# Perceiver layer on one core: group sums on ScalarE, context loads in pairs, a fifth-slot load in order of use, and the last two k-tiles by batch

## The chip, the cores and the metric

One Trainium2 chip, one core. The metric is device time of the whole program in microseconds, the median of several runs. The kernel is written out by hand: every engine has its own list of instructions, and semaphores tie the lists together.

## The reference, cut to what matters

Two batches of 128 rows with 2048 features go through three residual steps: a quantised product with a context, multi-query attention with 32 heads, and a linear layer with 4-bit weights in groups of 128 inputs.

```python
def _L0_xattn_ref(x1, x2, x1_scale, x1_zp, x2_scale, x2_zp):
    q1 = fake_quant(x1, x1_scale, x1_zp)
    q2 = fake_quant(x2, x2_scale, x2_zp)
    return jnp.matmul(q1, q2)

def _L0_attn_ref(hidden_states, Wq, Wkv, Wo):
    q = (hidden_states @ Wq).reshape(b, s, NUM_HEADS, HEAD_DIM)
    kv = hidden_states @ Wkv
    ...
    attn = jax.nn.softmax(scores, axis=-1)
    out = jnp.einsum('bhqk,bkd->bqhd', attn, v).reshape(b, s, h)
    return out @ Wo

def _L0_ffn_ref(x, qweight, qzeros, scales, bias):
    wq = qweight[:, None, :] >> shifts[None, :, None] & MASK
    wq = wq.reshape(IN_FEATURES, OUT_FEATURES)
    zq = _unpack4(qzeros, OUT_FEATURES) + 1
    W = scales[g_idx] * (wq - zq[g_idx]).astype(scales.dtype)
    return jnp.einsum('bsi,io->bso', x, W) + bias

x = x + _L0_xattn_ref(_layernorm(x), ctx_4096, ...)     # ctx_4096 is (2, 2048, 2048) f32
x = x + _L0_attn_ref(_layernorm(x), Wq, Wkv, Wo)
x = x + _L0_ffn_ref(_layernorm(x), qweight, qzeros, scales, bias)
```

## The kernel before, in words

The program has four stages, one after the other on TensorE.

**Context stage.** The context is 32 k-tiles of 128 rows by 2048 columns, 1 MiB each, 16 for each batch. SyncE loads them into a ring of eight slots (`ctx_slots`: four in `raw`, four in `ctx_more`; line 299), each as soon as ScalarE has rounded the tile that lay there (`ctx_q`). ScalarE rounds a tile to uint8 in `round_ctx` (L434), VectorE turns it into bf16 in `convert_ctx` (L699, two buffers `q16`), TensorE multiplies it in `ctx_tile` (L978, four products of 512 columns, and L985, four column sums). Between these ScalarE also quantises the rows of x (`quantise_rows`), and for batch 0, while batch 1 still streams, takes the square root for the second norm (`sqrt_of(2)`) and copies four transposed blocks out of PSUM (`upper(0, g)`, L447). After the last tile come the zero-point product, the residual, the norm and the transposes of batch 1 (`transposes(1)`, L1010).

**Query stage.** The products that want full f32 accuracy are made of three: each operand is split into an upper part (ScalarE, rounded to fp32r: `upper`, `upper_w`) and a remainder (VectorE: `remainder`, `remainder_w`), and TensorE computes upper x upper, upper x lower, lower x upper. The weights come in granules of 1 MiB (four k-tiles by 512 columns; `load_granule`), numbered `w`: 0 to 15 are Wq, 16 to 31 are Wo, 32 to 47 are the k-tiles of the linear layer. Attention for the eight (head group, batch) units runs between the granules of Wq (scores L1104, transposed probabilities L1116, values L1128, `heads_hi` L498 and `heads_lo` L830).

**Output stage.** Sixteen granules of Wo, `o_granule(i, b)` (L1017, L1018, L1019). Raw, upper and lower parts have five slots here; the fifth is `raw_fifth` with room in `xt`. The list `USED` has the granules in the order in which TensorE finishes them: 16, 17, 18, 20, 19, 21, ... TensorE runs `o_granule(4, 0)` (w = 20, fifth slot) before `o_granule(3, 0)` (w = 19), but the loads, ScalarE's upper parts and VectorE's remainders go 19, 20.

**Linear layer.** The weight is never built as a whole: VectorE unpacks two nibbles at a time (`nibbles(m)`, L878), ScalarE subtracts eight (`less_eight(m)`, L574), VectorE multiplies by the upper and the lower part of the scales (`ffn_upper(j)` L885, `ffn_lower(j)` L890), and TensorE runs `f_granule(j, b)`: for each k-tile j and batch b eight products by the upper part (`f_by_upper`) and four by the lower (`f_by_lower`), all in L1166. What the zero points and the bias add is one more product of eight (`correction`, L1199) of `corr_r` with `rsum`, the sums of the normed rows over each group of 128 inputs. Before, those sums come from TensorE: `row_sums` (L1160) multiplies the 16 transposed k-tiles of both parts with a 0/1 mask `group_of`, and VectorE and ScalarE combine and split the result (L945, L946, L594, L948). The normed rows lie in `work`, which is also where `nibbles(1)` and `nibbles(2)` write once the transposes have read it. `corr_split` is signalled when `corr_r` is made (L920).

The last lines of TensorE's list run k-tiles 12 to 15 for batch 0 and then for batch 1, the last of each with one bank after the other finished, so that VectorE can add (L959) and SyncE can store (L345).

## Time and profile before

| | before |
|---|---|
| median of 3 runs | 416.29 us (416.13 to 417.54) |
| the profiled execution | 416.08 us |
| its span in the profile | 414.3 us |
| mean granted TensorE clock | 0.984 of full |
| TensorE busy | 369.8 us (89%) |
| VectorE busy | 315.9 us (76%) |
| ScalarE busy | 222.6 us (54%) |
| GpSimd busy | 18.9 us (5%) |
| HBM read | 74.91 MB |

The profile is of one execution. Busy time of matmuls is modelled and overlaps by up to 0.17 us from one to the next, so the distance between two starts is the better price. The shares of busy time are means over stages that have different limits; the rows further down are taken stage by stage.

### The profile page before, as it was taken

Reading aid. Unit: us, or ns where it says so; the run is one execution under the profiler, and the core shown is the slowest. Engines: PE = TensorE matmul, PEld = TensorE weight load, DVE = VectorE, ACT = ScalarE, POOL = GpSimd, SP = SyncE. Lnnn points to the kernel's source line nnn. Section 1 sums busy time; section 2 is a strip of 40 time slices with the busy share of each in tenths; the row PEclk is TensorE's granted clock in tenths of the full one; section 3 lists DMA queues with packets and bytes.
Section 4 is the critical chain, followed back from the end, with each engine's and each line's share of the span. In section 5 each row is a group of like instructions: output and inputs, shape, how many; then the busy total and the mean of one; then the engine's idle time right before and its main releaser. Section 6 shows DMA issues by size and latency. Waiting matters only on the chain.

```text
span 414.3 us, 4696 instructions
## 1 busy us (share of the span) xinstructions
PE 369.8 (89%) x1828; PEld 269.2 (65%) x1828; DVE 315.9 (76%) x359; ACT 222.6 (54%) x266; POOL 18.9 (5%) x51
## 2 busy tenths in 40 slices
PE   0167768779899999999999999999999999999996
PEld 0112223227687777777877777888888788888884
DVE  2598989858853693783984977995999899999922
ACT  1898988986344576576675735544524433333000
POOL 6000000008000000000020000000000000000000
PEclk9998986999999999999999999999999999999999
DMA  8999999997173594685349421967200000000033
GB/s 324 422 424 422 415 425 422 416 400 283 27 277 115 184 223 122 209 180 173 130 142 277 139 95 53 356 224 277 111 0 0 2 0 0 2 0 2 0 101 101
DMA packets 24274, 77.44 MB, mean 187 GB/s; under 512 B 1626, under 2 KB 1802, under 8 KB 19210
## 3 DMA queue, kind: packets, MB, share of 16 engines
q1 hardware_dynamic: 24084, 77.01, 51.4%
q8 instruction: 14, 0.23, 0.3%
q10 hardware_dynamic: 168, 0.13, 0.1%
q14 instruction: 8, 0.07, 0.1%
HBM read 74.91 MB, written 2.10 MB: 186 GB/s over the span
## 4 chain that ended last, share of the span: by engine, by line
PE 71%; DVE 12%; DMA 10%; ACT 3%; issue 2%; ACTq 0%; DVEq 0%
PE bank L1166 20%; PE bank L1017 12%; PE bank L1019 12%; PE bank L1018 12%; DMA ctx_more<-in_ctx 9%; DVE q L699 3%; ACT q L434 2%; PE bank L1030 2%; PE bank L1128 2%; PE bank L1104 2%; DVE stats L613 2%; PE bank L1116 1%; PE bank L1040 1%; DMA prm_row<-in_L_xattn_x_zp 1%; PE bank L1010 1%
## 5 line engine op out<-in xcount | busy, mean ns | idle before, releaser
L456 ACT ACTIVATE w_hi<-raw 128x2048 fp32r<-128x2048 f32 x29 | 55.4, 1914 | 35.9 <-DMA raw<-in_L_attn_Wo 15.7
L643 DVE TENSOR_TENSOR w_lo<-raw,w_hi 128x2048 fp32r<-128x2048 f32 x27 | 61.6, 2286 | 11.2 <-ACT w_hi L456 11.2
L978 PE MATMUL bank<-q,at 128*128 128x512 bf16 x128 | 39.4, 438 | 15.0 <-DVE q L699 14.5
L1166 PE MATMUL bank<-w_hi,hd 128*128 128x512 f32 x208 | 52.6, 390 | 0.0
L1166 PEld LDWEIGHTS bank<-w_hi,hd 128*128 128x128 f32 x208 | 39.0, 188 | 8.0
L699 DVE TENSOR_SCALAR q<-q 128x2048 bf16<-128x2048 uint8 x32 | 38.4, 1217 | 5.4 <-ACT q L434 2.8
L1017 PE MATMUL bank<-w_hi,hd 128*128 128x512 f32 x104 | 41.2, 396 | 0.0
L1019 PE MATMUL bank<-w_hi,hd 128*128 128x512 f32 x104 | 40.5, 390 | 0.0
L1018 PE MATMUL bank<-w_lo,hd 128*128 128x512 f32 x104 | 40.5, 389 | 0.0
L1017 PE MATMUL bank<-w_hi,xt 128*128 128x512 f32 x96 | 39.6, 412 | 0.0
L1019 PE MATMUL bank<-w_hi,xt 128*128 128x512 f32 x96 | 37.6, 392 | 0.0
L1018 PE MATMUL bank<-w_lo,xt 128*128 128x512 f32 x96 | 37.5, 390 | 0.0
L485 ACT ACTIVATE work<-work,neg_mx 128x128 f32<-128x128 f32 x64 | 24.8, 389 | 23.4 <-DVE neg_mx L811 23.3
L434 ACT ACTIVATE q<-raw,prm,inv 128x2048 uint8<-128x2048 f32 x16 | 33.1, 2091 | 3.3 <-DMA raw<-in_ctx 3.3
L434 ACT ACTIVATE q<-ctx_more,prm,inv 128x2048 uint8<-128x2048 f32 x16 | 33.0, 2089 | 3.0 <-DMA ctx_more<-in_ctx 3.0
L978 PEld LDWEIGHTS bank<-q,at 128*128 128x128 bf16 x128 | 11.1, 106 | 34.8 <-DVE q L699 18.3
L574 ACT ACTIVATE work<-work 128x4096 bf16<-128x4096 uint16 x5 | 18.1, 3617 | 21.2 <-DVE work L878 21.2
L1166 PE MATMUL bank<-w_lo,hd 128*128 128x512 f32 x104 | 28.8, 389 | 0.0
L803 DVE SCALAR_TENSOR_TENSOR work<-kq,bank 128x128 f32<-128x128 f32 x64 | 13.3, 280 | 17.6 <-PE bank L1104 17.6
L1017 PEld LDWEIGHTS bank<-w_hi,hd 128*128 128x128 f32 x104 | 19.5, 188 | 4.9 <-issue 0.8
L1017 PEld LDWEIGHTS bank<-w_hi,xt 128*128 128x128 f32 x96 | 18.0, 188 | 6.5 <-issue 2.6
L1019 PEld LDWEIGHTS bank<-w_hi,hd 128*128 128x128 f32 x104 | 19.5, 188 | 4.2
(157 smaller groups left out, 618.8 us busy)
## 6 DMA issues: line engine op xcount, KB each, us to landing
raw<-in_ctx SPq DMA_DIRECT2D x16, 1024.0 KB, 17.1
ctx_more<-in_ctx SPq DMA_DIRECT2D x16, 1024.0 KB, 17.7
raw<-in_L_attn_Wq SPq DMA_DIRECT2D x16, 1024.0 KB, 5.7
raw<-in_L_attn_Wo SPq DMA_DIRECT2D x13, 1024.0 KB, 5.1
raw_fifth<-in_L_attn_Wo SPq DMA_DIRECT2D x3, 1024.0 KB, 7.2
resid<-in_x SPq DMA_DIRECT2D x2, 1024.0 KB, 11.7
scale<-in_L_ffn_scales SPq DMA_DIRECT2D x16, 128.0 KB, 6.1
packed<-in_L_ffn_qweight SPq DMA_DIRECT2D x2, 1024.0 KB, 7.1
```

The costliest lines, as they stand in the source:

```text
L434: nc.scalar.activation(q8[:, i % Q8], ctx_slots[i % CTX_RING], ACT.Identity, bias=prm[:, 3:4], scale=inv[:, 2:3]).then_inc(ctx_q, 1)
L456: nc.scalar.activation(hi_slots[s], raw_slots[s], ACT.Copy).then_inc(w_hi_set, 1)
L485: ins = nc.scalar.activation(prob[:, c], prob[:, c], ACT.Exp, scale=-1.0, bias=neg_mx[:, u % 2, h:h + 1], accum_out=den[:, u % 2, h:h + 1])
L574: nc.scalar.activation(values.bitcast(BF16), values.bitcast(U16), ACT.Copy, bias=-8.0).then_inc(d8_set, 1)
L643: nc.vector.tensor_tensor(lo_slots[s], raw_slots[s], hi_slots[s].bitcast(F32), ALU.subtract).then_inc(w_lo_set, 1)
L699: nc.vector.tensor_scalar(q16[:, i % 2], q8[:, i % Q8], -QSHIFT, None, ALU.add).then_inc(ctx_c, 1)
L803: ins = nc.vector.scalar_tensor_tensor(out=prob[:, c], in0=kq[:], scalar=-sl[2 * PAIRS * g + r], in1=bank[:, SCORE_BANK + r % 2, r // 2 * ...
L978: mm(bank[:, 4 * b + n, :], at[:, k, b * P:(b + 1) * P], q16[:, i % 2, n * CH:(n + 1) * CH], start=start, stop=False)
L1017: mm(bank[:, out_bank, :], x_hi, hi[:, c], start=first, stop=False)
L1018: mm(bank[:, out_bank, :], x_hi, lo[:, c], start=False, stop=False)
L1019: return mm(bank[:, out_bank, :], x_lo, hi[:, c], start=False, stop=last)
L1166: return mm(bank[:, 4 * b + n, :], left[:, j, b * P:(b + 1) * P], right[slot_of(W_F + j)][:, n * CH:(n + 1) * CH], start=part == 0 and j = ...
```

## The change

It has five parts.

1. **Group sums.** `row_sums` with its mask goes. ScalarE now copies each group of 128 columns of the normed rows onto itself with a running sum (`group_sums`), 16 instructions for each batch, then writes that batch's 16 sums twice more into the columns of the second and third block. TensorE transposes the two 128x128 arrays (`sums_transposed`), VectorE splits the result. GpSimd makes two columns of ones in place of the mask.
2. **Order at the start of the linear layer.** Batch 1 of k-tiles 0 to 2 is done for three of the four banks first, since bank 7 receives the sums; the fourth chunk follows when the sums have been read. `nibbles(1)` moves ahead into `packed[:, 1]`, whose own load therefore waits for k-tile 3's lower part; `corr_r` is made earlier.
3. **Context in pairs.** Two k-tiles a transfer, 2 MiB: partition p of pair t takes rows 2p and 2p+1, so each partition's piece is 16 KiB in one run in place of 8 KiB. The transposes of `a16` take every second column to match. The last pair goes as two single transfers.
4. **Fifth slot.** The loads, the upper parts and the remainders of Wo follow `USED`: w = 20 before w = 19.
5. **Last k-tiles.** Only k-tiles 14 and 15 run batch by batch at the end.

```diff
+        group_sum = sb("group_sum", [P, B, P], F32)
-        nib_slots = [nib_a[:], work[:, 0], work[:, 1]]
+        nib_slots = [nib_a[:], packed[:, 1], work[:, 0]] + [(nib_a[:], work[:, 1], work[:, 0])[m % 3]
+                                                           for m in range(3, NPAIR)]
+        ctx_pair_slots = [t[:, s:s + 2] for t in (raw, ctx_more) for s in (0, 2)]
...
+        def sum_copies(b):
+            return group_sum[:, b, CBLK:3 * CBLK].rearrange("p (k c) -> p k c", k=2)[:, :, 0:GROUPS]
+        def sums_twice(b):
+            return group_sum[:, b, 0:GROUPS].unsqueeze(1).to_broadcast([P, 2, GROUPS])
...
-            for i in range(CTX_TILES):
-                if i == 6:
+            for i in range(CTX_TILES // 2 - 1):
+                s = i % len(ctx_pair_slots)
+                if i == 3:
                     sp.dma_start(resid[:, 1, :], x[1]).then_inc(x_loaded[1], 16)
-                if i >= CTX_RING:
-                    sp.wait_ge(ctx_q, i - CTX_RING + 1)
-                sp.dma_start(ctx_slots[i % CTX_RING], ctx_tiles[i]).then_inc(ctx_loaded[i % CTX_RING], 16)
+                if 2 * i >= CTX_RING:
+                    sp.wait_ge(ctx_q, 2 * i - CTX_RING + 2)
+                sp.dma_start(ctx_pair_slots[s], ctx_pairs[i]).then_inc(ctx_loaded[s], 16)
+            for e in range(2):
+                i = CTX_TILES - 2 + e
+                sp.wait_ge(ctx_q, i - CTX_RING + 1)
+                sp.dma_start(ctx_slots[i % CTX_RING], ctx_pairs[i // 2, :, e]).then_inc(ctx_last[e], 16)
...
-                load_granule(wo_rows, W_O, w)
+                load_granule(wo_rows, W_O, USED[w])
...
+            sp.wait_ge(f_lo_set, 4)
             sp.dma_start(packed[:, 1, :], qweight[P:2 * P, :]).then_inc(packed_loaded[1], 16)
...
+            def group_sums(b, groups):
+                for g in groups:
+                    rows = work[:, b, g * GROUPSIZE:(g + 1) * GROUPSIZE]
+                    ins = nc.scalar.activation(rows, rows, ACT.Copy, accum_out=group_sum[:, b, g:g + 1])
+                if g == GROUPS - 1:
+                    ins.then_inc(rs_sum, 1)
+                    act.wait_ge(rs_sum, b + 1)
+                    nc.scalar.activation(sum_copies(b), sums_twice(b), ACT.Copy).then_inc(rs_rows, 1)
+
             less_eight(0)
+            less_eight(1)
             sqrt_of(4)
             for g in range(4):
                 upper(2, g)
-            less_eight(1)
+            act.wait_ge(masks_set, 1)
+            group_sums(0, range(12))
             sqrt_of(5)
+            group_sums(0, range(12, GROUPS))
             for g in range(4):
                 upper(3, g)
-            act.wait_ge(rs_sum, 1)
-            nc.scalar.activation(rsum_t.bitcast(F32R), rtmp, ACT.Copy).then_inc(rs_set, 1)
-            for m in range(2, NPAIR):
+            group_sums(1, range(GROUPS))
+            less_eight(2)
+            for m in range(3, NPAIR):
                 less_eight(m)
...
-            dve.wait_ge(rs_done, 1)
-            link(nc.vector.tensor_scalar(rtmp, bank[:, 7, 0:B * P], one_row[:], None, ALU.add))
-            nc.vector.tensor_tensor(rtmp, bank[:, 7, B * P:2 * B * P], rtmp, ALU.add).then_inc(rs_sum, 1)
-            dve.wait_ge(rs_set, 1)
-            nc.vector.scalar_tensor_tensor(out=rsum[:], in0=rsum_t, scalar=part_lo[:, 1:2], in1=rtmp,
-                                           op0=ALU.mult, op1=ALU.add).then_inc(rs_out, 1)
             for j in range(3, KT):
                 ffn_upper(j)
+                if j == 3:
+                    dve.wait_ge(rs_done, 1)
+                    nc.vector.tensor_copy(rsum_t.bitcast(F32R), bank[:, 7, 0:B * P]).then_inc(rs_set, 1)
+                    dve.wait_ge(rs_set, 1)
+                    nc.vector.scalar_tensor_tensor(out=rsum[:], in0=rsum_t, scalar=part_lo[:, 1:2],
+                                                   in1=bank[:, 7, 0:B * P], op0=ALU.mult,
+                                                   op1=ALU.add).then_inc(rs_out, 1)
                 ffn_lower(j)
...
-            def row_sums():
-                pe.wait_ge(masks_set, 3)
+            def sums_transposed():
+                pe.wait_ge(rs_rows, B)
                 pe.wait_ge(lo_out, 4 * B + UNITS + 8)
-                for k in range(KT):
-                    ins = mm(bank[:, 7, :], group_of[:, k // PACK, :], hd[:, :, k, :], start=k == 0, stop=k == KT - 1)
+                for b in range(B):
+                    ins = nc.tensor.transpose(bank[:, 7, b * P:(b + 1) * P], group_sum[:, b, :], ident[:])
                 ins.then_inc(rs_done, 1)
...
-            f_by_upper(2, 0, (0,))
-            row_sums()
-            f_by_upper(2, 0, (1,))
+            f_by_upper(2, 0)
+            f_granule(0, 1, range(NCH - 1))
             f_by_lower(2, 0)
-            pe.wait_ge(rs_sum, 1)
-            f_granule(0, 1)
+            f_granule(1, 1, range(NCH - 1))
+            sums_transposed()
+            f_granule(2, 1, range(NCH - 1))
             pe.wait_ge(rs_out, 1)
+            for j in range(3):
+                f_granule(j, 1, range(NCH - 1, NCH))
             pe.wait_ge(corr_split, 1)
             correction()
-            f_granule(1, 1)
-            f_granule(2, 1)
-            for j in range(3, KT - 4):
+            for j in range(3, KT - 2):
                 f_granule(j, 0)
                 f_granule(j, 1)
             for b in range(B):
-                for j in range(KT - 4, KT - 1):
-                    f_granule(j, b)
+                f_granule(KT - 2, b)
                 f_last_granule(b)
```

How the lists change at three places. First TensorE, behind the transposes of batch 1's normed rows (`transposes(3)`), from the second of k-tile 2's products for batch 0 on. L1166 and L1190 are the linear layer's products, L1160 the group sums by product, L1184 the transposes of the sums, L1199 and L1223 the correction. Before:

```order
L1166 MATMUL bank<-w_hi,hd 128x512 x3
L1160 MATMUL bank<-hd,group_of 128x512 [waits lo_out,masks_set]
L1160 MATMUL bank<-hd,group_of 128x512 x15
L1166 MATMUL bank<-w_hi,hd 128x512 [waits lo_out,f_hi_set]
L1166 MATMUL bank<-w_hi,hd 128x512 x3
L1166 MATMUL bank<-w_lo,hd 128x512 [waits f_lo_set]
L1166 MATMUL bank<-w_lo,hd 128x512 x3
L1166 MATMUL bank<-w_hi,hd 128x512 [waits lo_out,f_hi_set,rs_sum]
```

After:

```order
L1190 MATMUL bank<-w_hi,hd 128x512 x7
L1190 MATMUL bank<-w_hi,hd 128x512 [waits lo_out,f_hi_set]
L1190 MATMUL bank<-w_hi,hd 128x512 x5
L1190 MATMUL bank<-w_lo,hd 128x512 [waits f_lo_set]
L1190 MATMUL bank<-w_lo,hd 128x512 x2
L1190 MATMUL bank<-w_lo,hd 128x512 [waits f_lo_set]
L1190 MATMUL bank<-w_lo,hd 128x512 x3
L1190 MATMUL bank<-w_hi,hd 128x512 [waits lo_out,f_hi_set]
L1190 MATMUL bank<-w_hi,hd 128x512 x5
L1190 MATMUL bank<-w_lo,hd 128x512 [waits f_lo_set]
L1190 MATMUL bank<-w_lo,hd 128x512 x2
L1184 MATMUL bank<-ident,group_sum 128x128 [waits lo_out,rs_rows]
```

Sixteen products of 512 columns, which stood behind four products of k-tile 2, are gone; two transposes stand behind thirty products.

Second, ScalarE from the first `less_eight` on (L574 and L583; L447 and L454 copy transposed blocks, L427 and L431 take the square root, L597 sums a group, L601 writes the copies). Before:

```order
L574 ACTIVATE nib_a<-nib_a 128x4096 [waits nib_set]
L427 ACTIVATE sd<-mv,eps_col 128x1 [waits var_set]
L447 ACTIVATE hd<-bank 128x4x128 [waits tr_done] x4
L574 ACTIVATE work<-work 128x4096 [waits nib_set]
L427 ACTIVATE sd<-mv,eps_col 128x1 [waits var_set]
L447 ACTIVATE hd<-bank 128x4x128 [waits tr_done] x4
L594 ACTIVATE k_t<-kv_t 128x256 [waits rs_sum]
L574 ACTIVATE work<-work 128x4096 [waits nib_set]
```

After:

```order
L583 ACTIVATE nib_a<-nib_a 128x4096 [waits nib_set]
L583 ACTIVATE packed<-packed 128x4096 [waits nib_set]
L431 ACTIVATE sd<-mv,eps_col 128x1 [waits var_set]
L454 ACTIVATE hd<-bank 128x4x128 [waits tr_done] x4
L597 ACTIVATE work,group_sum<-work 128x128 [waits masks_set]
L597 ACTIVATE work,group_sum<-work 128x128 x11
L431 ACTIVATE sd<-mv,eps_col 128x1 [waits var_set]
L597 ACTIVATE work,group_sum<-work 128x128 x4
L601 ACTIVATE group_sum<-group_sum 128x2x16 [waits rs_sum]
L454 ACTIVATE hd<-bank 128x4x128 [waits tr_done] x4
L597 ACTIVATE work,group_sum<-work 128x128 x16
L601 ACTIVATE group_sum<-group_sum 128x2x16 [waits rs_sum]
```

The second `less_eight` has moved ahead of the transposes; 32 sums and two copies stand behind them.

Third, VectorE between the last four attention units (L803 and L824 add the position bias, L811 and L832 find the maxima, L643 and L664 are remainders of weights). Before:

```order
L811 TENSOR_REDUCE neg_mx<-work 128x8 [waits score_out]
L643 TENSOR_TENSOR w_lo<-raw,w_hi 128x2048 [waits w_hi_set]
L803 SCALAR_TENSOR_TENSOR work<-kq,bank 128x128 [waits pt_done,score_done]
L803 SCALAR_TENSOR_TENSOR work<-kq,bank 128x128 x7
L811 TENSOR_REDUCE neg_mx<-work 128x8 [waits score_out]
L816 RECIPROCAL rden<-den 128x8 [waits exp_done]
L818 TENSOR_TENSOR work<-work,rden 128x1024 [waits dve_step]
L643 TENSOR_TENSOR xt<-raw_fifth,xt 128x2048 [waits w_hi_set]
```

After:

```order
L832 TENSOR_REDUCE neg_mx<-work 128x8 [waits score_out]
L664 TENSOR_TENSOR xt<-raw_fifth,xt 128x2048 [waits w_hi_set]
L824 SCALAR_TENSOR_TENSOR work<-kq,bank 128x128 [waits pt_done,score_done]
L824 SCALAR_TENSOR_TENSOR work<-kq,bank 128x128 x7
L832 TENSOR_REDUCE neg_mx<-work 128x8 [waits score_out]
L837 RECIPROCAL rden<-den 128x8 [waits exp_done]
L839 TENSOR_TENSOR work<-work,rden 128x1024 [waits dve_step]
L664 TENSOR_TENSOR w_lo<-raw,w_hi 128x2048 [waits w_hi_set]
```

The remainder of the fifth-slot granule and that of granule 19 have changed places.

## Rows read from the trace of the kernel before

**Rows 1.** Busy time by stretch: us, each engine's busy (count), granted clock, DMA, GB/s

```profile
44.00:93.40 49.40, 37.22 (x212) 13.05 (x212) 41.48 (x49) 44.26 (x26) 0.00 (x0) 0.90 1.02 416
127.00:250.00 123.00, 121.88 (x655) 92.38 (x654) 83.69 (x123) 76.04 (x177) 2.13 (x2) 1.00 0.57 168
```

**Rows 2.** The chain of waits in order of time: start, us, what

```profile
51.34 17.74 DMA ctx_more<-in_ctx
...
88.98 2.10 ACT q L434
...
334.25 74.13 PE bank L1166 x327
```

**Rows 3.** ScalarE's timeline, context stage: start, us, line, operation, idle before and releaser

```profile
45.17 6.14 ACT L434 ACTIVATE q<-ctx_more,prm,inv 128x2048 uint8<-128x2048 f32 x3
51.70 2.09 ACT L434 ACTIVATE q<-raw,prm,inv 128x2048 uint8<-128x2048 f32 x1 [0.39 <-DMA raw<-in_ctx]
...
71.59 2.10 ACT L434 ACTIVATE q<-raw,prm,inv 128x2048 uint8<-128x2048 f32 x1 [0.40 <-DMA raw<-in_ctx]
73.60 1.06 ACT L447 ACTIVATE xt<-bank 128x512 fp32r<-128x512 f32 x2
74.55 2.09 ACT L434 ACTIVATE q<-raw,prm,inv 128x2048 uint8<-128x2048 f32 x1
...
97.13 1.92 ACT L456 ACTIVATE w_hi<-raw 128x2048 fp32r<-128x2048 f32 x1 [0.80 <-DMA raw<-in_L_attn_Wq]
99.83 1.92 ACT L456 ACTIVATE w_hi<-raw 128x2048 fp32r<-128x2048 f32 x1 [0.77 <-DMA raw<-in_L_attn_Wq]
```

**Rows 4.** TensorE's timeline in the output stage, at the first fifth-slot granule

```profile
238.58 0.50 PE L1017 MATMUL bank<-xt,hd 128*128 128x512 f32 x1 [1.04 <-DVE xt L643]
```

**Rows 5.** VectorE's timeline, the remainders of granules 19 and 20

```profile
229.84 2.28 DVE L643 TENSOR_TENSOR w_lo<-raw,w_hi 128x2048 fp32r<-128x2048 f32 x1
236.24 2.28 DVE L643 TENSOR_TENSOR xt<-raw_fifth,xt 128x2048 fp32r<-128x2048 f32 x1
```

**Rows 6.** TensorE's timeline, start of the linear layer

```profile
320.13 1.95 PE L1010 MATMUL bank<-ident,work 128*128 128x128 f32 x16
321.84 1.17 PE L1166 MATMUL bank<-w_hi,hd 128*128 128x512 f32 x4
324.03 3.87 PE L1160 MATMUL bank<-hd,group_of 128*128 128x512 f32 x16 [1.02 <-DVE hd L634]
327.74 1.07 PE L1166 MATMUL bank<-w_hi,hd 128*128 128x512 f32 x4
```

**Rows 7.** VectorE's timeline, same place, and one `nibbles` further on

```profile
321.40 2.48 DVE L634 TENSOR_TENSOR hd<-bank,hd 128x512 fp32r<-128x512 f32 x4 [0.25 <-ACT hd L447]
323.80 2.28 DVE L890 TENSOR_TENSOR w_lo<-work,scale 128x2048 fp32r<-128x2048 bf16 x1
...
338.58 1.22 DVE L878 TENSOR_SCALAR nib_a<-packed 128x2048 int32<-128x2048 int32 x1
```

**Rows 8.** ScalarE's timeline: two of the exponentials with a sum, and batch 1's upper parts

```profile
200.39 0.40 ACT L485 ACTIVATE work<-work,neg_mx 128x128 f32<-128x128 f32 x1 [6.23 <-DVE neg_mx L811]
200.70 0.19 ACT L485 ACTIVATION_READ_ACCUMULATOR work<-work,neg_mx 128x1 f32 x1
200.79 0.39 ACT L485 ACTIVATE work<-work,neg_mx 128x128 f32<-128x128 f32 x1
...
320.77 2.07 ACT L447 ACTIVATE hd<-bank 128x512 fp32r<-128x512 f32 x4 [3.85 <-PE bank L1010]
```

**Rows 9.** TensorE by stretch: us, busy (count), granted clock, DMA, GB/s

```profile
39.20:42.40 3.20, 3.20 (x14) 0.50 1.02 425
...
60.00:70.00 10.00, 8.52 (x28) 0.51 1.01 421
```

**Rows 10.** TensorE's timeline around these stretches, and at `transposes(1)`

```profile
60.46 1.86 PE L978 MATMUL bank<-q,at 128*128 128x512 bf16 x4 [1.37 <-DVE q L699]
...
104.56 2.07 PE L1010 MATMUL bank<-ident,work 128*128 128x128 f32 x16 [0.64 <-DVE work L627]
```

More of the change, by code:

```diff
@@ L183, in perceiver @@
         wkv_loaded = sem("wkv_loaded")
-        ctx_loaded = [sem(f"ctx_loaded{s}") for s in range(CTX_RING)]
+        ctx_loaded = [sem(f"ctx_loaded{s}") for s in range(CTX_RING // 2)]
+        ctx_last = [sem(f"ctx_last{e}") for e in range(2)]
         w_loaded = [sem(f"w_loaded{s}") for s in range(RING + 1)]
@@ L430, in round_ctx @@
             def round_ctx(i):
-                act.wait_ge(ctx_loaded[i % CTX_RING], 16 * (i // CTX_RING + 1))
+                if i < CTX_TILES - 2:
+                    act.wait_ge(ctx_loaded[i // 2 % len(ctx_pair_slots)], 16 * (i // CTX_RING + 1))
+                else:
+                    act.wait_ge(ctx_last[i % 2], 16)
                 if i >= Q8:
@@ L871, in nibbles @@
                 dve.wait_ge(packed_loaded[h], 16)
-                if m == 1:
-                    dve.wait_ge(tr_done, 4 * 3)
-                elif m == 2:
-                    dve.wait_ge(tr_done, 4 * 4)
+                if m in (2, 4):
+                    dve.wait_ge(tr_done, 4 * (m // 2 + 2))
+                    dve.wait_ge(rs_sum, m // 2)
                 elif m >= 3:
                     dve.wait_ge(f_lo_set, 2 * (m - 3) + 2)
-                nc.vector.tensor_scalar(nib_slots[m % 3].bitcast(I32), packed[:, h, :], BITS * s, 0x000F000F,
+                nc.vector.tensor_scalar(nib_slots[m].bitcast(I32), packed[:, h, :], BITS * s, 0x000F000F,
                                         ALU.logical_shift_right, ALU.bitwise_and).then_inc(nib_set, 1)
@@ L912, in _ @@
             second_residual(1, 1)
-            for i in range(11, 15):
+            for i in range(11, 14):
                 remainder_w(W_O + i)
+            dve.wait_ge(corr_hi, 1)
+            nc.vector.scalar_tensor_tensor(out=corr_r[:], in0=corr_up.bitcast(F32), scalar=part_lo[:, 0:1],
+                                           in1=corr, op0=ALU.mult, op1=ALU.add).then_inc(corr_split, 1)
+            remainder_w(W_O + 14)
             nibbles(0)
+            nibbles(1)
             second_residual(2, 0)
@@ L918, in _ @@
             remainder_w(W_O + 15)
-            dve.wait_ge(corr_hi, 1)
-            nc.vector.scalar_tensor_tensor(out=corr_r[:], in0=corr_up.bitcast(F32), scalar=part_lo[:, 0:1],
-                                           in1=corr, op0=ALU.mult, op1=ALU.add).then_inc(corr_split, 1)
             dve.wait_ge(scale_set, HALVES)
@@ L932, in _ @@
                 remainder(2, g)
-            nibbles(1)
             ffn_lower(1)
@@ L1135, in o_granule @@
                 w = W_O + i
-                pe.wait_ge(w_lo_set, w - 1)
+                pe.wait_ge(w_lo_set, USED.index(w) - 1)
                 if n == 0:
@@ L1168, in f_part, with f_by_upper, f_by_lower, f_granule @@
                           start=part == 0 and j == 0, stop=part == 2 and j == KT - 1)
-            def f_by_upper(j, b, parts=(0, 1)):
+            def f_by_upper(j, b, chunks=range(NCH)):
                 pe.wait_ge(f_hi_set, j + 1)
                 pe.wait_ge(lo_out, 4 * B + UNITS + 4 * (b + 1))
-                for part in parts:
-                    for n in range(NCH):
+                for part in range(2):
+                    for n in chunks:
                         f_part(j, b, n, part)
-            def f_by_lower(j, b):
+            def f_by_lower(j, b, chunks=range(NCH)):
                 pe.wait_ge(f_lo_set, j + 1)
-                for n in range(NCH):
+                for n in chunks:
                     ins = f_part(j, b, n, 2)
-                if b == B - 1:
+                if b == B - 1 and n == NCH - 1:
                     ins.then_inc(w_used, 1)
-            def f_granule(j, b):
-                f_by_upper(j, b)
-                f_by_lower(j, b)
+            def f_granule(j, b, chunks=range(NCH)):
+                f_by_upper(j, b, chunks)
+                f_by_lower(j, b, chunks)
             def f_last_granule(b):
```

49 lines of the change are left out of this document (17 added, 32 removed).

## The prediction

> **What bounds the kernel now.** I read the busy time by stretch first. From 44 to 93 us the DMA engines are busy all the time, at 416 GB/s, while TensorE is busy 37 of 49 us; from 127 to 250 us TensorE is busy 121.9 of 123 us and the DMA engines half the time [rows 1]. So there are two regimes: the context stage waits for the stream, everything behind it for TensorE. The chain in order of time agrees: a context transfer, ScalarE's last rounding at 88.98, and from 334.25 on nothing but the products of L1166, 327 of them without a hole [rows 2]. An edit behind 127 us counts only for what it takes off TensorE's list or out of its waits; an edit in the context stage counts only if the last rounding ends at another time.
>
> **The change part by part.** Times are those of the profiled execution (416.08 us, of which 414.3 are the span).
>
> *Fifth slot in order of use.* TensorE stands 1.04 us before `o_granule(4, 0)`, released by the remainder of granule 20 [rows 4]. That remainder starts at 236.24; the one in its old place starts at 229.84 and is for granule 19, which TensorE wants only two granules later [rows 5]. Swapped, granule 20 is ready at 229.84 + 2.28 = 232.1, 5 us before its use, and granule 19 at 238.5. Gain **1.04**. What is late next: attention's units 6 and 7 wait for TensorE itself and move with it, and so do the loads of granules 24 and later, which wait for `w_used`. Bounds: 0, if another wait ends there just as late, and 1.04.
>
> *Sixteen products gone.* They start at 324.03 and the next product at 327.74: gain **3.71** [rows 6]. Two transposes of 128 columns come in; sixteen take from 320.13 to 321.84, so two cost **0.21**.
>
> *The wait ahead of them.* Four products of 0.227 (74.13 / 327 [rows 2]) from 321.84 end at 322.75; the sums waited for batch 1's last remainder until 324.03, a hole of 1.28 [rows 6, 7]. Now eight products stand there and cover 0.91 more: gain **0.90**. The hole of 0.38 stays.
>
> *New waits on TensorE.* I go on in the old clock, 1.04 to be taken off throughout. Nine products (batch 1 of k-tile 0, three banks) run from 324.03 to 326.07. Then `f_by_lower(2, 0)` wants k-tile 2's lower part: L890 starts at 323.80, 0.08 before the row ahead of it ends, so it really ends near 326.08 [rows 7] and the wait costs **0.1**. Four and nine products bring TensorE to 329.1, where the transposes want both batches' sums. ScalarE has copied batch 1's upper parts by 320.77 + 2.07 = 322.84 [rows 8]. Then it does 16 sums. The nearest row is the exponential with a sum over the same 128x128, one every 0.39 us (200.39 to 200.79), its accumulator read beside the next [rows 8]: 16 x 0.385 = 6.2, to 329.0, and half a microsecond for the self-wait, the copy and the last read, to 329.5. TensorE waits **0.4**. Bounds: nothing, if a plain copy is quicker than the exponential, and 16 x (0.39 + 0.19) = 9.3 in place of 6.2, if the reads do not overlap, which makes it 3.5.
>
> The Trainium skill has the price the other way: on the page "ScalarE: Activation LUTs", section "What ACT_TABLE_LOAD costs", an activation costs some 93 ns less without a bias operand, which the sums have not and the exponentials have. By that the sums would take 1.5 us less and the 0.4 would be nothing; no row here shows it, and the sum below keeps 0.4.
>
> Batch 0's sums cost nothing: twelve of them, 4.6 us, take the place of the second `less_eight`, which has moved to where ScalarE waited for the norm; four and the copy, 2 us, lie in the 3.85 us in which ScalarE was idle before L447 [rows 8]. If that cover failed, `sqrt_of(5)` and `upper(3, g)` would come late, and with them each product of batch 1. `rsum` has the nine products of k-tile 2 (2.0 us) to cover two VectorE instructions of under half a microsecond each. VectorE loses one `nibbles` and gets `corr_r` into a wait, so it runs ahead of TensorE by less than before, but never behind: two k-tiles cost it four instructions like L890 and one `nibbles`, 4 x 2.28 + 1.22 = 10.3 us at most [rows 7], and TensorE 48 x 0.227 = 10.9.
>
> *The load of `packed[:, 1]`* now waits for k-tile 3's lower part. `nibbles(4)` comes three k-tiles on, some 14 us later, and 1 MiB needs 2.5 us of an empty queue. Cost 0. *Last k-tiles:* the same products in another order; the last bank ends at the same place, and batch 0's stores still have 5.4 us (24 products) before batch 1's. Cost 0. *GpSimd's* shorter list is beside other work: 0.
>
> *Context in pairs.* Two opposite effects. (a) A tile waits for its partner. Eight tiles went by in 71.59 - 51.70 = 19.89 us, 2.486 each [rows 3]. ScalarE needs 2.03 for each, back to back ((6.14 - 2.09)/2 [rows 3]). Pair 12 (tiles 24, 25) is there when tile 25 was, 71.59 + 2.49 = 74.08. From there ScalarE has eight roundings, 16.2 us, and four `upper(0, g)`, 1.9 us (73.60 to 74.55, twice [rows 3]), and never catches up with the stream: end at 92.2 where it was 88.98 + 2.10 = 91.08 [rows 2]. That costs 1.15. (b) Pieces of 16 KiB in place of 8 KiB. A granule of Wq, in pieces of 2 KiB, takes 99.83 - 97.13 = 2.70 us for 1 MiB [rows 3]; the same with 8 KiB pieces 2.486. Over 16 engines that is 84.4 ns for 2 KiB and 310.8 for 8 KiB, hence 27.1 bytes a ns and about 9 ns for a piece. Four pieces fewer in each MiB: 0.036 us, and over the 26 MiB up to tile 25 0.95 us. Then pair 12 is there at 73.1 and the last rounding ends at 91.3. Net cost **0.2**. Bounds: 1.15 with no faster stream; with pieces free of cost (2.42 us for 1 MiB) the end is at 90.3, a gain of 0.8.
>
> **Sum:** -1.04 - 3.71 - 0.90 + 0.21 + 0.1 + 0.4 + 0.2 = **-4.7**. Profiled execution 411.4. The median of before lies 0.21 over its profiled run, so I forecast **411.6**.
>
> **The rivals.**
>
> *The stream is no faster in pairs* (rate set elsewhere than by the piece). For: 2.486 us is 422 GB/s, and both stretches of [rows 9] stand there (425 and 421), so 8 KiB may be enough. 1.0 us more: 412.6.
>
> *The clock falls at `transposes(1)`.* The granted clock fell to the lower level (1.2 GHz, 0.50) for 3.2 us from 39.2 and for about 10 us from 60 [rows 9], the second time right behind two holes, the last of 1.37 us [rows 10]. Before `transposes(1)` the hole is 0.64 [rows 10]. Its four granules of products still wait for Wq, while the norm comes 0.2 to 1.1 us later, so the hole grows to between 1 and 1.7. Low for 3.2 to 10 us costs half of it, 1.6 to 5: 413.2 to 416.6, the upper end at no change. Against: before it TensorE now works off a backlog and is busier.
> The Trainium skill ("TensorE: Matmul & The Clock Gate", section "Part 4: PE-mode transpose") says that a transpose does not count as busy the same way; by that the sixteen transposes there, 1.8 us, would lengthen the hole. The row at 104.56 neither shows nor excludes it.
>
> *The sums do not overlap their reads:* 3.1 us more, 414.7.
>
> *The change does not do what it says* in one place: the hole at `o_granule(4, 0)` stays, or VectorE, whose second norm of batch 0 comes 1 to 2 us later in pairs, does not catch up by the last tile. 1.0 to 1.3 more: 412.8.
>
> *Slower than before: pairs stream worse.* If a pair goes at the rate of the Wq granules, 2.70, the last tile comes 30 x 0.214 = 6.4 us later, ScalarE is then not the bound, and the sum is -4.9 + 6.4 = +1.5: 417.8. It decides from 0.16 us for each MiB. Against: the stretches stand at 416 GB/s whatever else the engines do, and longer runs have been quicker here, not slower.
>
> **How the numbers follow.** Forecast 0.39; stream no faster 0.22; clock 0.14; sums not overlapped 0.07; one part fails 0.14; pairs worse 0.04. Half a per cent, 2.1 us, is what a measurement of this kernel can tell from no change, so faster means under 414.2 and slower over 418.4. Faster: the first two, the fifth, a third of the clock case and little of the third, 0.81. Slower: pairs worse than 2.77 us for 1 MiB, or two mishaps together, 0.03. Same: 0.16. The range goes from 409.8 (pieces free of cost, sums hidden, and as much again for what the rows do not show) to 414.7, the sums' case.
>
> **What would show it.** In the profile of the changed kernel: no L1160; `o_granule(4, 0)` without a hole; transposes of the sums after a wait under 0.6 us; sums every 0.39 us; the last rounding of the context ending near 91.3 with a stream at 2.45 us for 1 MiB; `transposes(1)` near 104.8 at clock 1.00; the first product of k-tile 3 near 334.8; and no hole behind it. Wrong would be a last rounding beyond 92.5, a clock of 0.50 behind 100 us, or VectorE releasing TensorE behind 340 us.

## The result, and the profile after

The changed kernel takes 410.39 us (median of 4 runs, 410.31 to 410.53), the kernel before beside it 416.21 us (415.98 to 417.54). The ratio is 0.9854, 95% interval 0.9833 to 0.9875: 5.8 us less. The forecast was 411.6, its range 409.8 to 414.7. The profiled execution took 410.53 us, with a span of 408.7, 5.6 less than before.

Busy time by stretch, the same two as in [rows 1]:

```profile
44.00:93.40 49.40, 37.72 (x216) 13.77 (x212) 42.55 (x50) 44.96 (x28) 0.40 (x1) 0.90 1.01 419
127.00:250.00 123.00, 122.99 (x660) 93.52 (x661) 84.04 (x124) 77.19 (x179) 2.13 (x2) 1.00 0.57 168
```

The two regimes are the same. The context stage is still the stream's, at 419 GB/s in place of 416, but only up to 73 us, as ScalarE's rows below show. TensorE is now busy for 122.99 of 123 us behind it: the 1.1 us that were missing in [rows 1] are gone.

The chain of waits in order of time, its last row of products:

```profile
334.04 68.69 PE bank L1190 x303
```

`L1190` is the old `L1166` of [rows 2]. Its last unbroken stretch starts at 334.04 and has 303 products: TensorE has no hole from there to its last product.

TensorE's timeline at the start of the linear layer, which answers to [rows 6]:

```profile
318.61 1.95 PE L1034 MATMUL bank<-ident,work 128*128 128x128 f32 x16
320.32 3.82 PE L1190 MATMUL bank<-w_hi,hd 128*128 128x512 f32 x14
323.98 1.85 PE L1190 MATMUL bank<-w_lo,hd 128*128 128x512 f32 x7
325.66 1.55 PE L1190 MATMUL bank<-w_hi,hd 128*128 128x512 f32 x6
327.05 0.85 PE L1190 MATMUL bank<-w_lo,hd 128*128 128x512 f32 x3
327.74 0.38 PE L1184 MATMUL bank<-ident,group_sum 128*128 128x128 f32 x2
327.88 1.64 PE L1190 MATMUL bank<-w_hi,hd 128*128 128x512 f32 x6
...
333.88 3.33 PE L1190 MATMUL bank<-xt,hd 128*128 128x512 f32 x14
```

The distances between starts give the account. Fourteen products of 0.227 are 3.18 us, and the next row starts 3.66 later: 0.48 too much, at the hole before the remainders of batch 1. The ninth of them, the first product of batch 1, starts like this:

```profile
322.51 0.47 PE L1190 MATMUL bank<-w_hi,hd 128*128 128x512 f32 x1
```

It is 322.51 - 318.61 = 3.90 us behind the start of `transposes(3)`; the product that waited for the same remainders before was 324.03 - 320.13 = 3.90 behind it. So the hole is the 0.38 that is left of it behind the transposes (1.71) and eight products of 0.227, and the other 0.1 lies behind it: six products take 323.98 - 322.51 = 1.47 in place of 1.36. Seven products by the lower part take 1.68 in place of 1.59, 0.1 more. The transposes of the sums (`L1184`) start where the three products ahead end, without a wait, and take 0.14 for two. From `transposes(3)` to the first product of k-tile 3 it is 333.88 - 318.61 = 15.27 us; before it was 339.53 - 320.13 = 19.40. So 4.13 of the gain lie here, and 320.13 - 318.61 = 1.52 lie ahead of it.

ScalarE's timeline: the tiles from 53 us on, and the first group sums of batch 1. They answer to [rows 3, 8]:

```profile
53.48 4.08 ACT L441 ACTIVATE q<-raw,prm,inv 128x2048 uint8<-128x2048 f32 x2 [0.82 <-DMA raw<-in_ctx]
58.37 4.08 ACT L441 ACTIVATE q<-raw,prm,inv 128x2048 uint8<-128x2048 f32 x2 [0.81 <-DMA raw<-in_ctx]
...
73.06 2.09 ACT L441 ACTIVATE q<-raw,prm,inv 128x2048 uint8<-128x2048 f32 x1 [0.64 <-DMA raw<-in_ctx]
...
82.99 8.05 ACT L441 ACTIVATE q<-ctx_more,prm,inv 128x2048 uint8<-128x2048 f32 x4
...
321.18 0.33 ACT L597 ACTIVATE work<-work 128x128 f32<-128x128 f32 x1
321.38 0.22 ACT L597 ACTIVATION_READ_ACCUMULATOR work<-work 128x1 f32 x1
321.47 0.33 ACT L597 ACTIVATE work<-work 128x128 f32<-128x128 f32 x1
...
326.01 0.23 ACT L601 ACTIVATE group_sum<-group_sum 128x32 f32<-128x32 f32 x1
```

A pair comes every 4.89 us, 2.447 for each MiB from 53.48 to 73.06 (2.486 before). ScalarE waits for a context transfer last at 73.06; from there its own work is the bound. Its last rounding ends at 91.04, where it was 91.08. A group sum comes every 0.29 us.

### The profile page after: what moved, and what is told of

Read it like the earlier page. It is cut to its first block, busy times and chain, and to the rows that moved or that the text cites. A ratio compares the mean times of both kernels' runs of the same rounds, so it can differ in the third digit from the quotient of the medians.

```text
span 408.7 us, 4694 instructions
## 1 busy us (share of the span) xinstructions
PE 365.9 (90%) x1814; PEld 267.1 (65%) x1814; DVE 315.2 (77%) x358; ACT 230.7 (56%) x331; POOL 15.3 (4%) x31
## 4 chain that ended last, share of the span: by engine, by line
PE 74%; DMA 13%; ACT 5%; DVE 4%; issue 3%; ACTq 0%
PE bank L1190 21%; PE bank L1041 13%; PE bank L1043 13%; PE bank L1042 12%; DMA raw<-in_ctx 11%; ACT q L441 4%; PE bank L1054 2%; PE bank L1128 2%; PE bank L1152 2%; PE bank L1140 2%; DMA prm_row<-in_L_xattn_x_zp 1%; PE bank L1034 1%; PE bank L1064 1%; DVE stats L634 1%; PE bank L1113 1%
## 5 line engine op out<-in xcount | busy, mean ns | idle before, releaser
L664 DVE TENSOR_TENSOR w_lo<-raw,w_hi 128x2048 fp32r<-128x2048 f32 x27 | 61.6, 2285 | 10.6 <-ACT w_hi L465 10.5
L1190 PE MATMUL bank<-w_hi,hd 128*128 128x512 f32 x208 | 53.2, 391 | 0.1
L1190 PEld LDWEIGHTS bank<-w_hi,hd 128*128 128x128 f32 x208 | 38.8, 188 | 8.5 <-issue 0.5
L1190 PE MATMUL bank<-w_lo,hd 128*128 128x512 f32 x104 | 29.2, 390 | 0.0
L824 DVE SCALAR_TENSOR_TENSOR work<-kq,bank 128x128 f32<-128x128 f32 x64 | 13.3, 279 | 18.0 <-PE bank L1128 18.0
L583 ACT ACTIVATE work<-work 128x4096 bf16<-128x4096 uint16 x4 | 14.5, 3616 | 19.0 <-DVE work L899 19.0
```

What stands on the lines that cost most here:

```text
L583: nc.scalar.activation(values.bitcast(BF16), values.bitcast(U16), ACT.Copy, bias=-8.0).then_inc(d8_set, 1)
L664: nc.vector.tensor_tensor(lo_slots[s], raw_slots[s], hi_slots[s].bitcast(F32), ALU.subtract).then_inc(w_lo_set, 1)
L824: ins = nc.vector.scalar_tensor_tensor(out=prob[:, c], in0=kq[:], scalar=-sl[2 * PAIRS * g + r], in1=bank[:, SCORE_BANK + r % 2, r // 2 * ...
L1190: return mm(bank[:, 4 * b + n, :], left[:, j, b * P:(b + 1) * P], right[slot_of(W_F + j)][:, n * CH:(n + 1) * CH], start=part == 0 and j = ...
```

## The experiments

Ten kernels, each with the kernel before run beside it on the same chip. The first four ran on one chip, the next four on a second, the last two on a third, and the medians of the kernel before on these are 416.35, 416.07 and 416.38 us. The changed kernel itself has 410.39 (its first runs) and 410.49 (run again beside `both`, last below); it was not run beside the first eight. So a difference of 0.3 us or less between them and the changed kernel is not shown by the times alone, and the traces have to carry it. The diffs are against the changed kernel.

**The context tile by tile again**, everything else kept.

```diff
-    ctx_pairs = ctx_in.rearrange("b (t p e) n -> (b t) p e n", p=P, e=2)
+    ctx_pairs = ctx_in.rearrange("b (t e p) n -> (b t) p e n", p=P, e=2)
...
-            for i in range(CTX_TILES // 2 - 1):
+            for i in range(CTX_TILES):
...
+                sp.dma_start(ctx_slots[i % CTX_RING], ctx_pairs[i // 2, :, i % 2]).then_inc(ctx_loaded[i % CTX_RING], 16)
```

> The changed kernel with the context loaded one k-tile a transfer again, all else kept. My theory: the pairs' two effects cancel (a faster stream, 2.448 us for 1 MiB, against a ScalarE that gets its tiles two at a time and ends its last rounding at 91.05 us, as before at 91.08). So 410.4 plus 0 to 0.3 us, the stream at 2.486 us, the last rounding at 91.1 and ScalarE waiting 0.4 us for each of the last tiles. Rival: the pairs carry part of the gain beyond the forecast, then 411 or more.

410.66 us (410.54 to 410.92), ratio 0.9868 (0.9853 to 0.9883). By the times the pairs are worth 0.2 to 0.3 us, no more than the chips differ. The end of ScalarE's context stage:

```profile
88.96 2.09 ACT L432 ACTIVATE q<-ctx_more,prm,inv 128x2048 uint8<-128x2048 f32 x1 [0.40 <-DMA ctx_more<-in_ctx]
```

It waits for each of its last two tiles and ends at 91.05, where the pairs end at 91.04 without a wait. So the last rounding gains nothing. Yet `transposes(1)` starts at 104.59 here and at 104.37 in the changed kernel, 0.22 earlier. Up to the norm's first reciprocal the two traces go alike to 0.01 us. Then comes one VectorE instruction on 128x1. This kernel's GpSimd and VectorE:

```profile
93.72 9.21 POOL L410 TENSOR_TENSOR w_lo<-raw,w_hi 128x2048 fp32r<-128x2048 f32 x2 [87.72 <-ACT w_hi L456]
102.52 0.43 DVE L634 SCALAR_TENSOR_TENSOR nt<-nt,var,sd 128x1 f32<-128x1 f32 x1
```

The changed kernel's, and its TensorE:

```profile
93.00 9.21 POOL L416 TENSOR_TENSOR w_lo<-raw,w_hi 128x2048 fp32r<-128x2048 f32 x2 [86.97 <-ACT w_hi L465]
102.51 0.22 DVE L643 SCALAR_TENSOR_TENSOR nt<-nt,var,sd 128x1 f32<-128x1 f32 x1
104.37 2.08 PE L1034 MATMUL bank<-ident,work 128*128 128x128 f32 x16 [1.34 <-DVE work L648]
```

GpSimd makes the remainders of the first two granules of Wq. Tile by tile it is still at it when the VectorE instruction starts, and both end at 102.9; in pairs Wq arrives earlier, GpSimd is done at 102.2, and the instruction takes its usual 0.22. All twelve traces agree: in the four in which GpSimd is still at work there (before, `no_pairs`, `single8`, `both`) this instruction takes 0.39 to 0.45 us and ends within 0.03 of GpSimd; in the other eight it takes 0.22. The VectorE instructions before it, which run at their usual length while GpSimd works, read at most one array of SBUF beside PSUM and per-partition scalars; this one reads two. That this is the reason, no run shows. So 0.2 of the pairs' gain is this wait, and not the context's own chain.

**Pairs, but in pieces of 8 KiB**: two tiles a transfer as in the change, laid out as before.

```diff
-    ctx_pairs = ctx_in.rearrange("b (t p e) n -> (b t) p e n", p=P, e=2)
+    ctx_pairs = ctx_in.rearrange("b (t e p) n -> (b t) p e n", p=P, e=2)
...
-                                              a16[:, b].rearrange("m (t p e) -> m t e p", p=P, e=2)[:, k // 2, k % 2],
+                                              a16[:, b, k * P:(k + 1) * P],
```

> Pairs of 2 MiB, but each partition's two rows lie 128 rows apart, so the pieces are of 8 KiB as before; transposes in the old order of columns. If the rate hangs on the length of the piece, the stream is at 2.486 us for 1 MiB again and only the price of waiting for the partner is left: pair 12 is there at 74.1, the last rounding ends near 92.1, total 1.0 us over the changed kernel, 411.4. Rival: the rate comes from fewer and larger transfers, then 2.45 us and 410.4.

411.56 us (411.34 to 412.51), ratio 0.9893 (0.9878 to 0.9908). ScalarE's timeline:

```profile
59.30 4.08 ACT L441 ACTIVATE q<-raw,prm,inv 128x2048 uint8<-128x2048 f32 x2 [0.73 <-DMA raw<-in_ctx]
64.27 4.08 ACT L441 ACTIVATE q<-ctx_more,prm,inv 128x2048 uint8<-128x2048 f32 x2 [0.89 <-DMA ctx_more<-in_ctx]
...
84.55 8.04 ACT L441 ACTIVATE q<-ctx_more,prm,inv 128x2048 uint8<-128x2048 f32 x4
```

A pair every 4.97 us is 2.485 for each MiB, the pace of single tiles: the faster stream comes from the longer piece, not from fewer transfers. The last rounding ends at 92.6, 1.5 behind the single tiles (this profiled run, 412.51, is 0.95 over its kernel's median, so some of that is its own). This takes the two effects apart: pairing alone costs 411.56 - 410.66 = 0.9 us of time (both on one chip), the longer pieces give 1.1 to 1.2 back.

**Wo's fifth slot in the old order.**

```diff
-                load_granule(wo_rows, W_O, USED[w])
+                load_granule(wo_rows, W_O, w)
...
-                s = slot_of(USED[i])
-                dve.wait_ge(w_hi_set, i + 1)
+                s = slot_of(w)
+                dve.wait_ge(w_hi_set, w + 1)
...
-                pe.wait_ge(w_lo_set, USED.index(w) - 1)
+                pe.wait_ge(w_lo_set, w - 1)
```

> The changed kernel with loads, upper parts and remainders of Wo in the order 19, 20 again. Theory: the hole before the fifth-slot granule comes back whole, 1.3 us from start to start (236.50 to 238.58 before, where the same eight transposes elsewhere take 0.79), so 411.7. Rival, the size that the forecast used: 1.04 us, 411.4. A second rival: attention's waits behind it absorb part, under 411.2.

411.91 us (411.79 to 411.94), ratio 0.9896 (0.9882 to 0.9911). The hole of [rows 4] is back on TensorE:

```profile
236.43 1.04 PE L1138 MATMUL bank<-ident,work 128*128 128x128 f32 x8
238.51 0.50 PE L1039 MATMUL bank<-xt,hd 128*128 128x512 f32 x1 [1.05 <-DVE xt L662]
```

In the changed kernel's timeline the same eight transposes and the first product behind them:

```profile
236.33 1.04 PE L1140 MATMUL bank<-ident,work 128*128 128x128 f32 x8
237.12 0.47 PE L1041 MATMUL bank<-xt,hd 128*128 128x512 f32 x1
```

By starts it is 2.08 against 0.79 us: the hole is worth 1.29, not the 1.05 in brackets. The modelled end of the transposes (1.04 busy) lies 0.25 behind the start of what follows when nothing waits. In time the part is worth 1.4 to 1.5.

**The last four k-tiles by batch, as before.**

```diff
-            for j in range(3, KT - 2):
+            for j in range(3, KT - 4):
...
             for b in range(B):
-                f_granule(KT - 2, b)
+                for j in range(KT - 4, KT - 1):
+                    f_granule(j, b)
                 f_last_granule(b)
```

> The changed kernel with k-tiles 12 to 15 batch by batch again. Theory: nothing, 410.4, since the last k-tile's lower part ends at 389.8 and would be wanted near 391.0; VectorE leads by 1.2 us there. Rival: the last four k-tiles by batch leave VectorE behind TensorE, then TensorE stands before the last k-tile of batch 0 and the time is 411 or more.

410.48 us (410.3 to 411.85), ratio 0.9873 (0.9853 to 0.9892): no difference from 410.4 to 410.5. VectorE's last part of the weight in this kernel, and the first products of batch 0's last granule, which wait for it:

```profile
387.46 2.29 DVE L911 TENSOR_TENSOR w_lo<-work,scale 128x2048 fp32r<-128x2048 bf16 x1
```

```profile
390.92 0.62 PE L1190 MATMUL bank<-w_hi,hd 128*128 128x512 f32 x2
```

The part is ready at 389.75 and is wanted at 390.92, 1.2 us later. In the changed kernel it is ready at 389.8 and wanted at 396.44. So this part of the change buys slack that nothing uses in these traces.

**The group sums alone**: the edits of `no_pairs`, `no_fifth` and `old_tail` (the context, the fifth slot, the last k-tiles, above) together; only the group sums and the order around them are new.

> The kernel before with nothing but the new group sums and the new order at the start of the linear layer (context tile by tile, granules 19 and 20 in the old order, k-tiles 12 to 15 batch by batch). Theory: these carry what is left when the fifth slot's 1.3 to 1.5 us are taken off, so from the first product of the linear layer to k-tile 3's first product 4.1 us less than before, and 412.1. Rival: the parts help one another (the sums need the fifth slot's head start), then 413 or more.

412.10 us (411.85 to 414.85, 6 runs), ratio 0.9906 (0.9878 to 0.9933): 4.0 us less than the 416.07 beside it. With 1.4 to 1.5 for the fifth slot and 0.2 to 0.3 for the pairs that is 5.6 to 5.8, the whole gain. The profile fell on the run of 414.85, which is worth a look of its own. TensorE's timeline at the end of the context stage:

```profile
90.03 1.04 PE L991 MATMUL bank<-q,at 128*128 128x512 bf16 x4 [1.11 <-DVE q L709]
...
92.53 1.89 PE L991 MATMUL bank<-q,at 128*128 128x512 bf16 x4 [1.13 <-DVE q L709]
...
94.89 3.78 PE L1043 MATMUL bank<-w_hi,xt 128*128 128x512 f32 x8
...
107.47 2.07 PE L1023 MATMUL bank<-ident,work 128*128 128x128 f32 x16 [1.33 <-DVE work L637]
```

And TensorE by stretch there:

```profile
84.00:92.00 8.00, 5.90 (x37) 1.75 (x36) 4.99 (x5) 6.45 (x4) 0.00 (x0) 1.00 1.02 397
92.00:100.00 8.00, 7.47 (x22) 4.61 (x23) 2.73 (x5) 5.62 (x4) 6.10 (x2) 0.57 1.06 402
```

Behind two holes of 1.1 us the granted clock falls from 1.00 to the lower level, 1.2 GHz: the eight products from 94.89 on take 3.58 us, where the same eight take 1.94 at 2.4 GHz in the kernel before (93.69 to 95.63). `transposes(1)` starts at 107.47 in place of 104.56 [rows 10], and the run is 2.75 over its median. Everything behind goes at the usual pace: 338.24 - 323.00 = 15.24 us for the start of the linear layer, as in the changed kernel. So a fall of the clock at the end of the context stage can happen and costs what the clock rival said, in one run of six, and at the last tiles, not at `transposes(1)`. But the holes alone do not bring it about. The kernel before has the same two:

```profile
89.90 1.04 PE L978 MATMUL bank<-q,at 128*128 128x512 bf16 x4 [1.11 <-DVE q L699]
...
92.39 1.04 PE L978 MATMUL bank<-q,at 128*128 128x512 bf16 x4 [1.12 <-DVE q L699]
```

Its granted clock is 1.00 from 84 to 100 us. What decides between the two is not shown.

**The last eight k-tiles as single transfers** (in the layout of pairs, 8 KiB pieces), so that ScalarE need not wait for a partner where it can no longer make it good.

```diff
-            for i in range(CTX_TILES // 2 - 1):
+            for i in range((CTX_TILES - SINGLE) // 2):
...
-            for e in range(2):
-                i = CTX_TILES - 2 + e
+            for e in range(SINGLE):
+                i = CTX_TILES - SINGLE + e
```

> The changed kernel with the last eight k-tiles as single transfers in place of the last two, so that ScalarE has tile 24 before tile 25 is there. Theory: in pairs ScalarE is the bound from pair 12 on, eight roundings and four copies in a row; with tile 24 there 2.4 us earlier it starts after tile 23, near 72.4, and ends its last rounding near 90.5 in place of 91.05. VectorE and TensorE follow 0.6 us behind, so 0.5 us less: 409.9. Rival: VectorE and TensorE have a backlog of their own there, then 410.4.

409.96 us (409.72 to 410.67), ratio 0.9847 (0.9824 to 0.987): 0.4 to 0.5 under the changed kernel. ScalarE's timeline and TensorE's:

```profile
82.22 8.05 ACT L442 ACTIVATE q<-ctx_more,prm,inv 128x2048 uint8<-128x2048 f32 x4
```

```profile
103.77 2.07 PE L1035 MATMUL bank<-ident,work 128*128 128x128 f32 x16 [0.73 <-DVE work L649]
```

ScalarE's last rounding ends at 90.27 in place of 91.04, 0.77 earlier, and `transposes(1)` starts 0.6 earlier (104.37 in the changed kernel). The rest is the VectorE instruction of `no_pairs`: it takes 0.40 us again, since GpSimd ends only at 102.1 and the norm now comes before that.

**`transposes(3)` four products earlier**, since a hole of 0.48 was left for batch 1's remainders.

```diff
-            f_granule(1, 0)
+            f_by_upper(1, 0)
             transposes(3)
+            f_by_lower(1, 0)
             f_by_upper(2, 0)
```

> The changed kernel with transposes(3) ahead of the four products by k-tile 1's lower part. The norm is there 1.2 us before the transposes start, so they can go 0.9 us earlier, and ScalarE's upper parts and VectorE's remainders with them, until VectorE's upper part of k-tile 2 stands in the way (0.3 us). Theory: the hole before batch 1's first product shrinks from 0.5 to 0.2 us, 410.1. Rival: nothing, because VectorE is the bound there, 410.4.

410.05 us (409.89 to 410.19), ratio 0.9848 (0.9823 to 0.9873). TensorE's timeline, then VectorE's:

```profile
317.40 1.95 PE L1034 MATMUL bank<-ident,work 128*128 128x128 f32 x16
...
320.13 3.40 PE L1190 MATMUL bank<-w_hi,hd 128*128 128x512 f32 x14
323.36 1.82 PE L1190 MATMUL bank<-w_lo,hd 128*128 128x512 f32 x7
...
333.23 5.15 PE L1190 MATMUL bank<-xt,hd 128*128 128x512 f32 x22
```

```profile
317.06 2.28 DVE L906 TENSOR_TENSOR w_hi<-packed,scale_hi 128x2048 fp32r<-128x2048 bf16 x1
319.26 2.48 DVE L655 TENSOR_TENSOR hd<-bank,hd 128x512 fp32r<-128x512 f32 x4
```

Fourteen products now take 3.23 us: the hole is gone, and so is the slow product behind it. The four products that moved behind the transposes are 0.91 us, so the distance to k-tile 3, 333.23 - 317.40 = 15.83, compares with 15.27 + 0.91 = 16.18: a gain of 0.35, and 0.3 to 0.4 in time. (`transposes(1)` starts at 104.16 in this trace, 0.2 before the changed kernel's, which is no work of this edit.) More is not to be had by moving the transposes further ahead: VectorE goes from `ffn_upper(2)` straight into the remainders, without a wait between.

**The sums with a bias operand**: the same sums, `Identity` with a column of zeros in place of `Copy`.

```diff
-                    ins = nc.scalar.activation(rows, rows, ACT.Copy, accum_out=group_sum[:, b, g:g + 1])
+                    ins = nc.scalar.activation(rows, rows, ACT.Identity, bias=zero_col[:], accum_out=group_sum[:, b, g:g + 1])
```

> The changed kernel with each group sum as an identity with a bias column of zeros in place of a plain copy; the sums are the same. Theory: the bias column makes the distance between sums 0.385 us, as in the exponentials, in place of 0.293, so batch 1's sums end 1.5 us later, the transposes of the sums wait 0.3 to 0.5 us, and the total is 410.8. Rival: the exponential's longer distance came from its function or something else, then sums stay at 0.29 us and the time at 410.4.

410.55 us (410.49 to 410.87), ratio 0.986 (0.9838 to 0.9883). ScalarE's timeline, then TensorE's:

```profile
321.01 0.42 ACT L599 ACTIVATE work<-work,zero_col 128x128 f32<-128x128 f32 x1
321.39 0.42 ACT L599 ACTIVATE work<-work,zero_col 128x128 f32<-128x128 f32 x1
...
327.33 0.23 ACT L603 ACTIVATE group_sum<-group_sum 128x32 f32<-128x32 f32 x1
```

```profile
326.85 0.84 PE L1192 MATMUL bank<-w_lo,hd 128*128 128x512 f32 x3
327.61 0.44 PE L1186 MATMUL bank<-ident,group_sum 128*128 128x128 f32 x2
```

A sum comes every 0.385 us (321.01, 321.39, 321.78), the pace that the forecast had from the exponentials, and the copy comes 1.3 us later. TensorE's wait is there, but only 0.08 (0.76 for three products in place of 0.68), and from `transposes(3)` to k-tile 3 it is 333.83 - 318.44 = 15.39 us in place of 15.27. The time is 0.1 to 0.2 higher, which alone would show nothing. So the longer distance was sized rightly and its effect was not: TensorE gets to the transposes 0.1 us before the sums are there, not 0.4. The edit changes the function (`Copy` to `Identity`) and the operand together; what it shows is that the exponential's function is not needed for the longer distance.

**Both**: single transfers for the last eight k-tiles and the earlier `transposes(3)`.

> The changed kernel with both edits that helped: the last eight k-tiles as single transfers and transposes(3) ahead of k-tile 1's lower part. They lie in different stages, so theory: their gains add, 0.45 and 0.35 us, and the time is 409.6. Rival: the second is absorbed when everything ahead of it moves, 410.0.

409.59 us (409.46 to 410.24), ratio 0.9828 (0.9794 to 0.9861), against 416.38 for the kernel before and 410.49 for the changed kernel on the same chip. The slowest of its runs, 410.24, is below the fastest of the changed kernel's, 410.42. The two gains, 0.5 and 0.4, add up to 0.9: they lie one behind the other on the chain, in the context stage and at the start of the linear layer. This version beats both kernels.

**The changed kernel again**, beside the last one.

> The changed kernel itself once more, on the same chip as the one beside it, for the comparison: 410.4 us.

410.49 us (410.42 to 410.72), ratio 0.9848 (0.9809 to 0.9887). Its median repeats to 0.1 us.

## Why the prediction was right, point by point

The forecast was -4.7 and the time fell by 5.8; the sign, the likeliest case and the range held. The profiled executions are 5.55 apart, so 0.9 are owed by the terms. Three of the four erred to the same side:

| term | forecast | measured |
|---|---|---|
| fifth slot | -1.04 | -1.3 in the trace, -1.4 to -1.5 in time |
| start of the linear layer | -3.90 | -4.13 in the trace, -4.0 in time |
| context in pairs | +0.2 | -0.19 at `transposes(1)`, -0.2 to -0.3 in time |
| last k-tiles | 0 | 0 |

*Fifth slot.* The step held, `no_fifth` shows it: granule 20's remainder now starts at 229.67, and attention and the later granules moved along. The size was read from the wrong figure, the idle time in brackets, 1.04; the distance of the two starts in [rows 4] and of the same transposes elsewhere (206.94 to the next, 0.79) would have given 1.3.

*Products and transposes.* 3.71 for the products stands. The two transposes cost 0.14 to the next start, and the six products behind them 0.1 more than usual (327.88 to 329.35, 1.47 for 1.36): the forecast was 0.21, and 0.25 came.

*The hole before the remainders.* Forecast 0.38, and 0.38 it is: 3.90 us from `transposes(3)` to the product behind the hole, before and after. The products behind it then take 0.1 more than usual, which the forecast did not have; `tr3_early` closes the hole with four products more, and there the fourteen take 3.23.

*The sums.* Forecast 0.4 of waiting at 0.385 a sum; a sum takes 0.293 and nobody waits. This is the term that failed: the nearest row was the exponential, which has a bias operand, and the sums have none. `sums_bias` brings the 0.385 back without the exponential. Even so the wait was 0.08: counted from the start of `transposes(3)`, TensorE came 0.1 later than reckoned (9.09 for 8.97) and the sums 0.2 earlier (9.17 for 9.37).
The Trainium skill ("ScalarE: Activation LUTs", section "What ACT_TABLE_LOAD costs") states about 93 ns less without a bias operand. Here it is 385 - 293 = 92 ns, so the trace agrees; that it is the operand and not `Copy` against `Identity`, no run here takes apart.

*Context in pairs.* Both effects were there, and nearly as large as reckoned: in time pairing costs 0.9 (forecast 1.15; it would be 1.1 without the 0.2 that the VectorE instruction gives back, 0.22 us long in `pairs_8k` and 0.43 in `no_pairs`), and the longer pieces give 1.1 to 1.2 (forecast 0.95). Pair 12 came at 73.06 (forecast 73.1), and the stream went at 2.447 for each MiB (forecast 2.45). What was off is the end. ScalarE's eight roundings took 16.07 us in place of 16.2 (91.04 - 73.06, less 1.91 for the four copies), and with the rounded figures of the forecast that makes 91.04 in place of 91.3: net 0.04 gained, not 0.2 lost. And TensorE started `transposes(1)` 0.19 earlier, not 0.04, by the VectorE instruction that no longer ran until GpSimd's end (0.39 us before, 0.22 now). The forecast had nothing of that; this much of the pairs' gain is luck. The hole before `transposes(1)` grew from 0.64 to 1.34, within the 1 to 1.7 of the clock rival, but for another reason: the norm came no later, and TensorE's products ended earlier, among other things because the wait of 0.39 for a granule of Wq (at 101.79 before) is gone.

*The rivals.* A stream no faster in pairs is excluded by the pace of 2.447, and a worse one too. The sums overlap their reads (a distance of 0.29 with a read of 0.2). No part failed. The clock stayed at 1.00 behind 90 us in the changed kernel, in spite of the hole of 1.34. But the rival was no invention: `sums_alone` shows such a fall behind 92 us and its price, though behind holes that in the kernel before brought none.

What stays open: of the 29 runs of the kernel before, six lie at 417.44 to 419.05, 1.1 to 3.0 us over their medians, which may be the same fall of the clock; none of them was profiled, so that isn't shown. The mean clock of a run doesn't tell it either: the 414.85 run of `sums_alone` has 0.988, as high as any of its others. Of the 35 runs with pairs in 16 KiB pieces, none is more than 1.4 over its median; that leans towards the pairs, but no run shows that they protect against it.

## What to carry to other kernels

Read a hole from the distance of the starts on both sides of it, against the same instructions where nothing waits; the idle time in brackets is measured from a modelled end and was a fifth too small here. When transfers are made larger, split the effect in two, the later arrival of what is first in the transfer and the faster stream, and keep small transfers for the last ones, where the consumer cannot catch up. Before pricing an activation from the nearest row, compare the operands too, not only shape and function. And when a gain does not show at the step where it was reckoned, compare the two traces instruction by instruction up to where they part: here that was one small VectorE instruction beside GpSimd.
